# A graph layer on one core: windows of 180 message rows for each node tile in place of 192

## The chip, the cores and the metric

The kernel runs on one NeuronCore of a Trainium2 chip. The metric is the device time of one execution in microseconds (us); lower is better. The core has TensorE (PE in the rows; PEld is its weight load), VectorE (DVE), ScalarE (ACT), GpSimd (POOL) and SyncE (SP), and 16 DMA engines that move data between the main memory (HBM) and the on-chip memory.

## What is computed

One message-passing layer on a graph of 50,000 nodes with 160 features and 50,000 edges, and a LayerNorm behind it. The edges come sorted by their destination `dst`.

```python
h = silu(edge_scalars @ (Wfc1 / sqrt(16)));  w = h @ (Wfc2 / sqrt(64))
f0 = x0 @ Wl1_0 * a * inv8;   f1 = einsum('num,uv->nvm', x1, Wl1_1) * a * inv32
e0, e1 = f0[edge_src], f1[edge_src]           # gather by source
mid0..mid3 = products of w, e0/e1 and edge_attr_sh
n_k = segment_sum(mid_k, edge_dst) / clip(count, 1)   # mean by destination
conv = [scal @ Wl2_s, vec @ Wl2_v] * a * inv96;  alpha = scal @ Wa * a * inv96
out = layernorm(x + sc(x) + alpha * conv)     # sc: x times Wsc0, Wsc1
```

All arithmetic is float32. For the given inputs the 391 tiles of 128 nodes that hold nodes receive 128 edges each in the mean (standard deviation 11), and the fullest of them 160, counted from `dst`.

## The kernel before

The program has two stages, one after the other, and a start-up.

**Edge stage** (`edge_steps`): the edges go in 392 tiles of 128, two tiles to a step. GpSimd gathers the source rows (L548), TensorE transposes them and forms the weights and products, and VectorE writes a message of 163 numbers for each edge (gate, 160 features, a count of 1, and in the column `LABEL` the destination). Four tiles of messages at a time are stored to `rows` in HBM (L386). Behind the messages `rows` holds a pad of one window whose labels are -1.

**Window starts.** In the start-up GpSimd makes index tables and the pads (L505 to L528, `more_constants`, called after the second pair's gathers), and VectorE works out for each tile of 128 nodes at which row of `rows` its messages start. A flag (`prepare_flag`) sends the program to a slow general path if some tile has more than `WINDOW` messages or if `dst` isn't sorted; otherwise windows are used.

**Node stage** (`node_steps`): the nodes go in 98 groups of `GROUP = 4` tiles. For each group g:

- SP, `load_windows` (L413 to L425): it reads the four starts from `start_i` into registers (L413), waits until the window buffer is free (`agg_done` of the group four before; `RING = 4` buffers), and issues four DMAs (L422), one for each tile. A window is `WINDOW = WC_ROWS * WP` = 3 * 64 = 192 rows of messages, put into 64 partitions of three rows: tiles 0 and 1 into partitions 0 to 63 (`side(0)`), tiles 2 and 3 into partitions 64 to 127 (`side(1)`). Then it waits for `pre_ready` and `ra_ready` of the group four before and loads the node rows `xin` two groups ahead (`load_nodes`, L404). After every second group it waits for `fin_ready` and stores 8 tiles of results (L482).
- GpSimd: products `xa` of node rows and node attribute (L585, L589); when the group's windows have landed, the labels less the tile's first node, `lab` (L597); and the sum `res` (L608) of the group three before.
- VectorE: `hot` (L1082), a 0/1 matrix: which node of the tile a window row belongs to. A label outside the tile gives a row of zeros. Also the counts, coefficients, `pre` (L1044) and the statistics of the LayerNorm.
- TensorE: transposes of `xa` (L705); the sum by destination (L716), 24 products to a group, one for each tile and each of the three rows of a partition, contracting over the 64 partitions of `side(h)`; the self connection (L726, L728).
- ScalarE: `xt`, `agg` (L800), `std`, `fin` (L809).

The order on each engine is that of the loops; the engines meet in semaphores. The change touches `WP` (and with it `WINDOW`, the four loads L422, the products L716, the pads), `side`, and `more_constants`.

Of the kernel before, what the change touches and what calls it, by code (L numbers as in the profile page):

```python
# [47 lines left out]
GATE, CNT, LABEL = 0, 1 + D, 2 + D  # L48
SW = 2 + D
AW = 3 + D  # L50
RCNT, GRA = SW, SW + 1
WP = 64
WC_ROWS = 3
WINDOW = WC_ROWS * WP

# [19 lines left out]
def gnn_kernel(nc, table, x_g, src_t, dst_t, dst_rows, sh_t, ea_t, weights, out):  # L75
# [21 lines left out]
    with ExitStack() as ctx:  # L97
        def sb(name, shape, dt=F32):
            return ctx.enter_context(nc.sbuf_tensor(name, shape, dt))

        def sem(name):
            return ctx.enter_context(nc.semaphore(name))
# [14 lines left out]
        zeros = sb("zeros", [P, FILL, AW])  # L117
        pads = sb("pads", [WP, WC_ROWS, AW])

# [49 lines left out]
        win = sb("win", [P, RING, 2, WC_ROWS, AW])  # L169
# [47 lines left out]
        pads_set = sem("pads_set")  # L217
# [123 lines left out]
            return RING * i + (b - behind + 1)  # L341

        def side(h):
            return slice(h * WP, (h + 1) * WP)

        def block_rows(ap, first):

# [4 lines left out]
        def _(sp):  # L352
# [59 lines left out]
            def load_windows(i, b):  # L412
                _, firsts = nc.values_load_multi_w_load_instructions(  # L413
                    start_i[0:1, bass.ds((RING * i + b) * GROUP, GROUP)],
                    engines=[mybir.EngineType.SP], min_val=0, max_val=BASE + NP - P,
                    skip_runtime_bounds_check_because="a start is a count of edges, or the first "
                    "of a tile's own rows")

                if group_has(i, b, RING):
                    sp.wait_ge(agg_done, groups(i, b, RING))  # L420
                for k, first in enumerate(firsts):
                    sp.dma_start(win[side(k // 2), b, k % 2].rearrange("p c w -> p (c w)"),  # L422
                                 rows[bass.ds(first, WINDOW), :].rearrange(
                                     "(p c) w -> p (c w)", c=WC_ROWS)
                                 ).then_inc(win_in[b], 16)  # L425
# [67 lines left out]
        def _(pool):  # L493
# [10 lines left out]
            def more_constants():  # L504

                for ap, pattern, base, mult in (
                        (column[:], [[1, P]], 0, 0),
                        (tile_base[:], [[GROUP * P, NG], [P, 2]], 0, 0),
                        (bound[:], [[P * P, CH]], 0, P),
                        (node_base[:], [[P, NT]], BASE, 0),  # L510
                        (g_label[:], [[1, ROWS // P]], 0, ROWS // P),
                        (g_spare[:], [[0, 1]], NP, 1)):
                    nc.gpsimd.iota(ap.bitcast(I32), pattern=pattern, base=base,
                                   channel_multiplier=mult).then_inc(iotas_set, 1)
                pool.wait_ge(iotas_set, 6)
                nc.gpsimd.iota(tile_base[side(1), :].bitcast(I32),
                               pattern=[[GROUP * P, NG], [P, 2]], base=2 * P,
                               channel_multiplier=0).then_inc(iotas_set, 1)
                pool.wait_ge(iotas_set, 7)
                nc.gpsimd.memset(pads[:], 0.0).then_inc(pads_set, 1)  # L520
                nc.gpsimd.memset(later_mask[:], 1.0).then_inc(pads_set, 1)
                pool.wait_ge(pads_set, 2)
                nc.gpsimd.memset(pads[:, :, LABEL], -1.0).then_inc(pads_ready, 1)

                nc.gpsimd.affine_select(out=later_mask[:], in_=later_mask[:],
                                        compare_op=ALU.is_gt, fill=0.0, base=0,
                                        pattern=[[1, P]], channel_multiplier=-1
                                        ).then_inc(mask_ready, 1)  # L528
# [24 lines left out]
            def find_windows():  # L553

                pool.wait_ge(at_tile_i_ready, 1)
                for c in range(CH):
# [4 lines left out]
                    ).then_inc(picked_in, 16)  # L561

            edge_steps(pool, step, {(0, 1): more_constants, (1, 3): find_windows})

            pool.wait_ge(prepared, 1)
# [49 lines left out]
        def _(pe):  # L615
# [82 lines left out]
            def step(i, b):  # L698
# [8 lines left out]
                if group_alive(i, b, 1):  # L707
                    b1 = (b - 1) % 2

                    pe.wait_ge(hot_ready, groups(i, b, 1))  # L710
                    if group_has(i, b, 3):
                        pe.wait_ge(agg_ready, groups(i, b, 3))
                    for k in range(2):
                        for c in range(WC_ROWS):
                            for h in range(2):
                                last = nc.tensor.matmul(  # L716
                                    agg_ps[b1][:, 2 * h + k, 0:SW], hot[side(h), b1, k, c, :],
                                    win[side(h), (b - 1) % RING, k, c, 0:SW],
                                    start=c == 0, stop=c == WC_ROWS - 1)
                    last.then_inc(agg_done, 1)  # L720

                    pe.wait_ge(xt_out, groups(i, b, 1))
                    if group_has(i, b, 2):
                        pe.wait_ge(pre_ready, groups(i, b, 2))
                    for k in range(GROUP):
                        nc.tensor.matmul(sca_ps[:, k, :], xt[:, b1, k, :],  # L726
                                         wy[:, W_SA - W_Y0:W_SB - W_Y0], start=True, stop=True)
                    last = nc.tensor.matmul(scb_ps.rearrange("p k w -> p (k w)"),  # L728
                                            xt[:, b1, GROUP, :],
                                            wy[:, W_SB - W_Y0:WC - W_Y0], start=True, stop=True)  # L730
                    last.then_inc(sc_ready, 1)
# [463 lines left out]
```

## Time and profile before

| | us |
|---|---|
| median of 3 runs (lowest, highest) | 1144.48 (1143.96, 1147.09) |
| the profiled execution, device time | 1144.21 |
| its span, first to last instruction | 1142.4 |
| edge stage with start-up, to the first window load | 695 |
| node stage, from there to the end | 447 |

Device time and span differ by 1.8 us. The profile page gives for each engine the busy time and, in 40 slices of 28.6 us, the busy share in tenths. A view of waits lists for how long an engine stood idle and what it waited for. A timeline lists the instructions in order of time; for SP (in the rows SPq) it shows the DMAs that it issues and how long each issue occupied it. "MB" and "GB/s" are those of all 16 DMA engines. L422 is line 422 of the kernel.

### The profile page before, as it was taken

How to read it: one execution, taken by the hardware profiler on the slowest of the kernel's cores; microseconds unless marked ns; L12 is line 12 of the kernel's file. 1: busy time of each engine (PE TensorE's matmuls, PEld its weight loads, DVE VectorE, ACT ScalarE, POOL GpSimd, SP SyncE). 2: the span in 40 equal slices, each digit the busy share in tenths (PEclk: the TensorE clock that was granted, in tenths of full speed). 3: DMA queues.
4: the chain of work that ended last, by engine and by line, in shares of the span. 5: the costliest groups of instructions: out<-in, count | busy, mean ns of one | idle time of the engine just before them, and what ended most of it. 6: DMA issues, size and time to landing. Idle time of an engine off the chain costs nothing.

```text
span 1142.4 us, 29298 instructions
## 1 busy us (share of the span) xinstructions
PE 1024.2 (90%) x8726; PEld 941.3 (82%) x8726; DVE 908.3 (80%) x3171; ACT 640.4 (56%) x1865; POOL 759.4 (66%) x906
## 2 busy tenths in 40 slices
PE   4769999999999999999999998998888898998894
PEld 4759989989989998888888997887777787887783
DVE  4757877878787877777777876888988888988885
ACT  1324343434343434344343433888888898988887
POOL 6635656656656555666655662879887888878983
PEclk9879999999999999999999999999999999999997
DMA  5653333333333333333333433799989999998993
GB/s 160 151 135 98 107 99 101 94 104 103 97 99 107 99 97 98 105 98 98 98 97 95 112 98 121 218 267 273 270 260 262 282 281 264 283 264 258 271 276 136
DMA packets 88772, 186.64 MB, mean 163 GB/s; under 512 B 17831, under 2 KB 49895, under 8 KB 88616
## 3 DMA queue, kind: packets, MB, share of 16 engines
q1 hardware_dynamic: 69672, 152.17, 43.9%
q0 software_dynamic: 18944, 32.60, 14.0%
q8 instruction: 72, 1.18, 0.4%
q14 instruction: 84, 0.69, 0.2%
HBM read 119.75 MB, written 64.95 MB: 162 GB/s over the span
## 4 chain that ended last, share of the span: by engine, by line
PE 52%; issue 15%; POOL 14%; DVE 8%; another core or an unknown queue 5%; ACT 3%; DMA 2%; SPq 0%; DVEq 0%; POOLq 0%; ACTq 0%
PE ps L657 14%; PE ps L670 8%; PE ps L647 7%; POOL xa L589 6%; POOL xa L585 5%; PE ps L665 4%; PE ps L716 4%; PE ps L645 3%; PE ps L636 3%; PE ps L630 3%; PE ps L667 2%; POOL res L608 2%; PE ps L726 2%; PE ps L627 2%
## 5 line engine op out<-in xcount | busy, mean ns | idle before, releaser
L548 POOL DMA_INDIRECT gat<-table,src_now x392 | 377.1, 962 | 272.0 <-issue 135.5
L657 PEld LDWEIGHTS ps<-h_sb,wt 128*128 128x128 f32 x1568 | 204.3, 194 | 46.7 <-issue 38.8
L769 ACT ACTIVATE z<-ps 128x130 f32<-128x130 f32 x196 | 54.9, 280 | 325.2 <-PE ps L670 301.9
L657 PE MATMUL ps<-h_sb,wt 128*128 128x128 f32 x1568 | 213.3, 280 | 19.3 <-DVE mid L884 18.6
L716 PE MATMUL ps<-win,hot 64*128 64x162 f32 x2352 | 192.1, 309 | 0.0
L809 ACT ACTIVATE fin<-res,shift,rstd 128x160 f32<-128x160 f32 x392 | 172.1, 511 | 28.1 <-DVE shift L1090 25.9
L716 PEld LDWEIGHTS ps<-win,hot 64*128 64x128 f32 x2352 | 167.8, 189 | 16.7 <-issue 16.4
L608 POOL TENSOR_TENSOR res<-agg,pre 128x640 f32<-128x640 f32 x98 | 151.2, 1543 | 10.9 <-ACT agg L800 10.7
L670 PE MATMUL ps<-wy,mid 128*128 128x161 f32 x784 | 151.4, 316 | 0.0
L881 DVE TENSOR_TENSOR mid<-ps,e_sb 128x256 f32<-128x256 f32 x196 | 82.1, 419 | 85.0 <-remote 46.0
L1082 DVE TENSOR_TENSOR hot<-column,lab 128x768 f32<-128x768 f32 x98 | 135.3, 1381 | 1.0 <-issue 0.5
L762 ACT ACTIVATE e_sb<-ps 128x384 f32<-128x384 f32 x196 | 97.5, 498 | 67.7 <-PE ps L647 65.5
L800 ACT ACTIVATE agg<-ps,coef 128x160 f32<-128x160 f32 x392 | 121.6, 396 | 22.3 <-DVE coef L1075 22.3
L907 DVE SCALAR_TENSOR_TENSOR msg<-ps,sha,z 128x161 f32<-128x161 f32 x392 | 132.9, 381 | 0.3 <-issue 0.3
L1044 DVE TENSOR_TENSOR pre<-ps,xin 128x512 f32<-128x512 f32 x196 | 86.6, 482 | 42.3 <-PE ps L728 41.6
L647 PE MATMUL ps<-t_sb,wt 128*128 128x256 f32 x392 | 118.9, 386 | 0.0
L750 ACT ACTIVATE t_sb<-ps 128x384 f32<-128x384 f32 x196 | 95.7, 488 | 38.6 <-PE ps L630 26.0
L670 PEld LDWEIGHTS ps<-wy,mid 128*128 128x128 f32 x784 | 114.1, 192 | 0.0
L726 PE MATMUL ps<-wy,xt 128*128 128x128 f32 x784 | 113.9, 288 | 0.0
L589 POOL TENSOR_TENSOR xa<-xin 128x512 f32<-128x512 f32 x98 | 113.1, 1154 | 0.0
L705 PE MATMUL ps<-ident,xa 128*128 128x128 f32 x490 | 72.5, 279 | 43.7 <-POOL xa L589 41.6
L726 PEld LDWEIGHTS ps<-wy,xt 128*128 128x128 f32 x784 | 95.3, 192 | 17.4 <-issue 15.1
(98 smaller groups left out, 1880.1 us busy)
## 6 DMA issues: line engine op xcount, KB each, us to landing
win<-rows SPq DMA_DIRECT2D x392, 122.2 KB, 3.9
rows<-msg SPq DMA_DIRECT2D x98, 326.0 KB
xin<-x_g SPq DMA_DIRECT2D x98, 322.0 KB, 5.0
out<-fin SPq DMA_DIRECT2D x49, 640.0 KB, 5.5
gat<-table,src_now POOLq DMA_INDIRECT x392
eas<-ea_t SPq DMA_DIRECT2D x5, 512.0 KB
wt<-weights SPq DMA_DIRECT2D x1, 945.5 KB
shs<-sh_t SPq DMA_DIRECT2D x1, 752.0 KB
```

Source lines behind the costliest of these rows:

```text
L548: pool.indirect_dma_start(out=gat[:, n, 0:XW], out_offset=None, in_=table, in_offset=bass.IndirectOffsetOnAxis(ap=src_now[:, n:n + 1], axis=0)
L589: nc.gpsimd.tensor_tensor(xa[:, b0, 0:GROUP, :], xin[:, n, :, 1:1 + P], xin[:, n, :, 0:1].broadcast_to([P, GROUP, P]), ALU.mult).then_inc( ...
L608: nc.gpsimd.tensor_tensor(res[:, slot], agg[:, b3], pre[:, b3], ALU.add).then_inc(res_ready, 1)
L647: nc.tensor.matmul(e_ps[:, 1:3, :].rearrange("p s e -> p (s e)"), wt[:, W_E1:W_E1 + P], t_sb[:, b1, 1:3, :].rearrange("p s e -> p (s e)"), ...
L657: last = nc.tensor.matmul(w_ps[:, c, :], wt[:, w:w + P], h_sb[:, b1, :], start=True, stop=True)
L670: last = nc.tensor.matmul(y_ps[:, s, 1 + MUL0:YW], mid[:, b2, 2 + s, :], wy[:, W_Y1 - W_Y0:W_SA - W_Y0], start=True, stop=True)
L716: last = nc.tensor.matmul(agg_ps[b1][:, 2 * h + k, 0:SW], hot[side(h), b1, k, c, :], win[side(h), (b - 1) % RING, k, c, 0:SW], start=c == ...
L726: nc.tensor.matmul(sca_ps[:, k, :], xt[:, b1, k, :], wy[:, W_SA - W_Y0:W_SB - W_Y0], start=True, stop=True)
L800: last = nc.scalar.activation(agg[:, b0, k, :], agg_ps[b0][:, k, 1:1 + D], ACT.Copy, scale=coef[:, b0, k:k + 1])
L809: last = nc.scalar.activation(fin[:, past, k, :], res[:, past, k, :], ACT.Identity, bias=shift[:, past, k:k + 1], scale=rstd[:, past, k:k ...
L907: last = nc.vector.scalar_tensor_tensor(out=msg[:, 2 * j3 + s, 0:1 + D], in0=y_ps[:, s, 0:Y_C], scalar=sha[:, j3, s, 0:1], in1=z[:, b1, s, :],
L1082: nc.vector.tensor_tensor(hot[:, b0].rearrange("p k c e -> p (k c) e"), column[:].unsqueeze(1).broadcast_to([P, 2 * WC_ROWS, P]), lab[:, b ...
```

## The change

A window gets 180 rows in place of 192: `WP` becomes 60, so 60 partitions of three rows. The second half still starts at partition 64 (`HALF`). Partitions 60 to 63 and 124 to 127 of the window buffers are written by no load any more; their labels are set to -1 once, since `lab` and `hot` are still worked out for all 128 partitions. The products contract over 60 rows. The limit of the flag becomes 180.

```diff
@@ -49,7 +49,8 @@
 SW = 2 + D
 AW = 3 + D
 RCNT, GRA = SW, SW + 1
-WP = 64
+HALF = 64
+WP = 60
 WC_ROWS = 3
 WINDOW = WC_ROWS * WP
 
@@ -341,7 +342,7 @@
             return RING * i + (b - behind + 1)
 
         def side(h):
-            return slice(h * WP, (h + 1) * WP)
+            return slice(h * HALF, h * HALF + WP)
 
         def block_rows(ap, first):
 
@@ -519,7 +520,8 @@
                 pool.wait_ge(iotas_set, 7)
                 nc.gpsimd.memset(pads[:], 0.0).then_inc(pads_set, 1)
                 nc.gpsimd.memset(later_mask[:], 1.0).then_inc(pads_set, 1)
-                pool.wait_ge(pads_set, 2)
+                nc.gpsimd.memset(win[:, :, :, :, LABEL], -1.0).then_inc(pads_set, 1)
+                pool.wait_ge(pads_set, 3)
                 nc.gpsimd.memset(pads[:, :, LABEL], -1.0).then_inc(pads_ready, 1)
```

## Rows read from the trace of the kernel before

**Rows 1.** The profile page: span, and busy tenths in 40 slices
```profile
span 1142.4 us, 29298 instructions
PE   4769999999999999999999998998888898998894
DVE  4757877878787877777777876888988888988885
ACT  1324343434343434344343433888888898988887
POOL 6635656656656555666655662879887888878983
DMA  5653333333333333333333433799989999998993
```
**Rows 2.** Busy time of each engine by stretch: edge stage, node stage, last stretch
```profile
300.00:500.00 200.00, 191.78 (x1487) 180.53 (x1487) 158.68 (x595) 80.60 (x238) 120.03 (x149) 1.00 0.37 101
765.00:1105.00 340.00, 303.06 (x3070) 269.28 (x3070) 299.75 (x949) 297.44 (x868) 284.81 (x315) 0.99 0.96 270
1105.00:1142.40 37.40, 20.45 (x208) 17.93 (x204) 22.97 (x82) 29.16 (x84) 19.18 (x19) 0.83 0.49 167
```
**Rows 3.** Waits, all engines, 765 to 1105 us: total, times, longest
```profile
POOL lab L597 <- DMA win<-rows: 46.1, 44, 2.9
PE ps L705 <- POOL xa L589: 36.8, 36, 2.5
DVE pre L1044 <- PE ps L728: 31.3, 37, 1.5
```
**Rows 4.** Waits of SP's queue, 765 to 1105 us: all there are
```profile
SPq L404 <- DVE pre L1044: 3.7, 11, 0.6
SPq L482 <- ACT fin L809: 0.8, 2, 0.4
```
**Rows 5.** Timeline of SP where nothing holds it back: start us, us
```profile
718.30 2.44 SPq L422 DMA_DIRECT2D win<-rows  x4
720.84 0.53 SPq L404 DMA_DIRECT2D xin<-x_g  x1
721.87 2.44 SPq L422 DMA_DIRECT2D win<-rows  x4
```
**Rows 6.** Timeline of SP in mid node stage
```profile
944.70 3.25 SPq L422 DMA_DIRECT2D win<-rows  x4
948.06 0.51 SPq L404 DMA_DIRECT2D xin<-x_g  x1
949.09 2.46 SPq L422 DMA_DIRECT2D win<-rows  x4
951.64 0.53 SPq L404 DMA_DIRECT2D xin<-x_g  x1
952.22 0.42 SPq L482 DMA_DIRECT2D out<-fin  x1
953.15 3.03 SPq L422 DMA_DIRECT2D win<-rows  x4
...
961.43 3.26 SPq L422 DMA_DIRECT2D win<-rows  x4
...
969.88 3.23 SPq L422 DMA_DIRECT2D win<-rows  x4
```
**Rows 7.** Line L422, 765 to 1105 us: issue ns min/median/max
```profile
L422 SPq DMA_DIRECT2D win<-rows x315: 468/471/1920, 765.1 to 1104.4; - x158
```
**Rows 8.** DMA view, 765 to 1105 us: packets by size, loads and stores
```profile
DMA packets 42238, 91.97 MB, mean 270 GB/s; under 512 B 6925, under 2 KB 27089, under 8 KB 42182
win<-rows SPq DMA_DIRECT2D x315, 122.2 KB, 4.0
xin<-x_g SPq DMA_DIRECT2D x79, 322.0 KB, 4.9
out<-fin SPq DMA_DIRECT2D x39, 640.0 KB, 5.6
```
**Rows 9.** Groups by line, PE, 750 to 1100 us: busy us, mean ns
```profile
L716 PEld LDWEIGHTS ps<-win,hot 64*128 64x128 f32 x1946 | 138.4, 188 | 13.8 <-issue 13.6 <-DVE hot L1082 0.2
L726 PEld LDWEIGHTS ps<-wy,xt 128*128 128x128 f32 x648 | 78.8, 192 | 14.4 <-issue 12.8 <-ACT xt L792 1.6
```
**Rows 10.** Page, products with nearly the same columns: busy us, mean ns
```profile
L716 PE MATMUL ps<-win,hot 64*128 64x162 f32 x2352 | 192.1, 309 | 0.0
L670 PE MATMUL ps<-wy,mid 128*128 128x161 f32 x784 | 151.4, 316 | 0.0
```
**Rows 11.** Timeline of GpSimd in the start-up: start us, us
```profile
8.54 0.95 POOL L548 DMA_INDIRECT gat<-table,src_now  x1 [0.30 <-issue]
...
12.14 0.50 POOL L520 MEMSET pads<- 64x489 f32 x1
12.59 0.42 POOL L521 MEMSET later_mask<- 128x128 f32 x1
13.06 0.10 POOL L523 MEMSET pads<- 64x3 f32 x1
13.12 1.29 POOL L525 TENSOR_SCALAR_AFFINE_SELECT later_mask<-later_mask 128x128 f32<-128x128 f32 x1
14.37 0.18 POOL L538 COPY src_now<-srcs 128x4 int32<-128x4 int32 x1
15.36 1.02 POOL L548 DMA_INDIRECT gat<-table,src_now  x1 [0.81 <-POOL src_now L538]
```
**Rows 12.** DMA issues of other shapes, by line: ns min/median/max
```profile
L399 SPq DMA_DIRECT2D start_row<-starts_dram x1: 266/266/266, 61.8 to 61.8; - x1
L386 SPq DMA_DIRECT2D rows<-msg x98: 332/332/833, 38.0 to 708.6; - x98
L365 SPq DMA_DIRECT2D heads_i<-dst_rows x1: 973/973/973, 3.3 to 3.3; - x1
```
**Rows 13.** Timeline of SP in the start-up, and the page's size of `wt`
```profile
1.28 0.42 SPq L359 DMA_DIRECT2D wt<-weights  x1
...
3.28 0.97 SPq L365 DMA_DIRECT2D heads_i<-dst_rows  x1
...
wt<-weights SPq DMA_DIRECT2D x1, 945.5 KB
```

## The prediction

> **What bounds the kernel now.** Read the page's slices first [rows 1]. For 24 of 40 slices, the edge stage, TensorE is at 9 and the DMA engines at 3; after that the DMA row stands at 8 to 9 to the end and all four engines stand at 8 or so. The change touches the edge stage only in its start-up, so the node stage is what matters. The view by stretch [rows 2] says the same in numbers: from 765 to 1105 us the 16 DMA engines are busy 0.96 of the time and move 270 GB/s, TensorE is busy 303 of 340 us, VectorE 300, ScalarE 297, GpSimd 285. No engine is full, so look at what they wait for [rows 3]: the longest wait is GpSimd's, 46.1 us for window loads, and the next ones (the transposes for `xa`, `pre` for the self connection) come behind it in the loop. So the windows are late. Why? Either SP issues them late because a buffer is not free, or SP itself is late, or the DMA engines are. The waits of SP's queue [rows 4] rule out the first: in 340 us SP waited 4.5 us for other engines. SP is therefore occupied with issuing all the time.
>
> Its timeline shows with what. Where nothing holds it back [rows 5], a group takes 721.87 - 718.30 = 3.57 us: four window loads 2.44 us, one node load 0.53 us, and about half a microsecond between the node load and the next window, in which the starts are read into registers. With the store of results (every second group) it is 953.15 - 949.09 = 4.06 us [rows 6]. The mean, 3.82 us, is SP's own work for a group. The real pace is 79 node loads, one a group [rows 8], in 340 us: 4.30 us. The missing 0.48 us is in the issues themselves: the median issue of a window load takes 471 ns but some take up to 1920 [rows 7], and the long quartets (3.25, 3.03, 3.26 and 3.23 us against 2.44) stand right behind the store of 640 KB [rows 6, 8]. I read this as SP pushing against full DMA queues, at a DMA share of 0.96. So two things in series set the pace: SP's issuing, 3.82 of 4.30 us, and the DMA engines, which take the rest. What the change does to either decides; the four computing engines have 11 to 16% of slack.
>
> **The change part by part.** The sum is made against the profiled execution, 1144.21 us, 0.3 us below the median of the runs.
>
> *Products over 60 rows.* The 24 products of a group keep their number and their columns. Does a shorter contraction make them faster? With 64 rows the weight load takes 188 ns, with 128 rows 192 [rows 9]; the product 309 ns for 162 columns over 64 rows, 316 for 161 over 128 [rows 10]. Halving the rows gave at most 7 ns, so a sixteenth less gives nothing. `hot` and `lab` keep their shapes, all 128 partitions.
>
> *The memset of the labels and its wait.* One GpSimd instruction of 128x24 numbers between L521 and L523. Its neighbours take 0.10 us (64x3) and 0.42 us (128x128) [rows 11]; I take 0.25. GpSimd has the gather of 15.36 us queued behind it, and the edge pipeline is being filled at that time, so nothing surely hides it: 0.1 to 0.5 us, once.
>
> *The window loads, bytes.* Each of the 392 loads loses 4 of 64 packets of three message rows (122.2 KB / 64 = 1956 bytes [rows 8]). For a group that is 16 packets, 31.3 kB of 4 * 122.2 + 322 + 320 KB = 1158 kB, 2.7% of the traffic. If time went by bytes, that is 31.3 kB at 270 GB/s = 0.116 us a group. But a load is done when its last engine is done, and a packet is not split. 64 packets over 16 engines are four for each; 60 packets leave at least one engine with four, and if each engine takes an equal number, 15 engines keep four and one gets none. Then the queues of 15 engines hold just what they held before, and they set the end. Bounds: 0 and -0.116 us a group. I take 0, since an equal division is the plain way to cut 60 equal packets, and a varied one is the rival below.
>
> Here a page bears on it. The Trainium skill, "DMA: Bandwidth & Descriptors", section on why a DMA increments its semaphore by 16, says that the descriptor generator picks the largest number of engines up to 16 that divides the row counts, and that with HWDGE these are always the lowest-numbered ones. By it the 60 rows go to 15 fixed engines and the 16th is idle for every window, so the gain from bytes would be 0; the opposite result, -0.116 us a group, is that of counting bytes. No row of this trace shows single DMA engines.
>
> *The window loads, issue.* This is the cost that the trace doesn't show: what SP needs to issue a load whose 60 rows don't divide by 16. All loads and stores of the node stage have 64 or 128 rows. Nearest rows [rows 12]: the one DMA of a single row took 266 ns, the message stores in an idle queue 332; the one DMA whose count is no multiple of 16, `heads_i` with 392 pieces, took 973 ns. So the price lies between 332 - 266 = 66 ns less and 973 - 420 = 553 ns more, where 420 is that of a plain issue within a burst (the store's in [rows 6]). `heads_i` was issued two microseconds behind a load of 945 KB [rows 13], and behind the 640 KB store the quartets wait as well, so much of its 973 ns may be waiting. I take +40 ns, near the 64-row load, because all else of the load is the same, and keep both ends. The same page says that the issuing sequencer itself writes the remaining increments when fewer than 16 engines take part; that would be an addition to each issue, and no run here has its price.
>
> *What of it reaches the end.* 4 * 0.04 = 0.16 us a group on SP. SP already stands still for 0.48 us a group against full queues; when it comes later, the queues have drained further and it stands less. That cover isn't perfect, since the standstill falls mostly on every second quartet and the DMA share is 0.96 and not 1. I take three quarters as covered: 0.04 us * 98 groups = 4 us. Without the cover it would be 16 us.
>
> Sum: 1144.2 + 0.25 (memset) + 0 (products) + 0 (bytes) + 4 (issue) = 1148.5, and its own range 1142 to 1154: the issue price from 0 to 60 ns with half to all of it covered, and a little from the engine or two with less to do.
>
> **The rivals.**
>
> *Bytes count.* If the DMA engines are slow together, because the memory or the way into the chip's memory is shared, then 2.7% less traffic helps whichever engine it is taken from. For it: the DMA share is full at 270 GB/s, whatever limits it. Against it: the equal division above, and that GpSimd, VectorE and TensorE need 285 to 303 us of the 340 themselves. Price: 0.116 us * about 90 groups that run at full DMA share = 10.4 us, so 1134. It can't go much further: SP's 3.82 us a group stays.
>
> *A dear issue (slower).* If issuing 60 rows costs over 0.48 / 4 = 0.12 us more than 64, SP's own work passes the present pace of 4.30 us and the cover is used up; from there each 0.1 us of price costs 0.4 us a group, 39 us in all. Place: L422, 392 times. At 0.2 us more: 3.82 + 0.80 = 4.62 us a group plus some standstill, 0.4 us * 98 = 39 us, so 1183. At the upper bound of 0.55 us: (2.20 - 0.48) * 98 = 169 us, 1313. For it: `heads_i`. Against it: 973 ns can be a full queue.
>
> *The change doesn't do what it says.* With a limit of 180 rows the flag would send the program to the general path if a tile had more. The fullest tile of these inputs has 160, so windows are used; I leave 1 in 100.
>
> **How the numbers follow.** My forecast, nothing from the bytes and a small, mostly covered price of the issue: 0.53, at 1148. Bytes count: 0.24, 1131 to 1141. A dear issue: 0.20, from 1155 up, half of it above 1178. Others: 0.03. A measurement of this kernel can tell about 0.3%, 3.4 us, from no change: 1141.1 to 1147.9 is the same. Of the forecast's 0.53 I put 0.35 there, 0.16 above and 0.02 below; bytes count gives 0.22 faster and 0.02 the same; the dear issue 0.20 slower. With the others: faster 0.25, same 0.38, slower 0.37. The range runs from the bytes case's 1132 to 1178 in the dear case; about 0.1 is left out above and 0.04 below. The forecast's own range is 1142 to 1154.
>
> **What the profile of the changed kernel would show.** The median issue of L422: 471 ns now; 500 to 530 if my price is right, over 600 for the dear issue, the same or less for none. The pace of node loads: 4.30 us now; 4.34 by the forecast, 4.19 if bytes count, 4.5 and up if the issue is dear. The quartets right behind a store should shrink by about what the others grow. DMA share: by the forecast the mean falls by about a sixteenth of the windows' part, since one engine idles, though nothing gets faster; if bytes count, GB/s stay near 270 and the share near 0.96. The wait for `win` grows with SP, or shrinks if bytes count. The products stay at 309 ns. I am wrong if the median issue is unchanged and the pace still moves: then the engines' queues, not SP, carry the change.

## The result, and the profile after

The changed kernel takes 1103.98 us (median of 4 runs, 1100.88 to 1113.02) against 1144.5; the ratio is 0.966, with a 95% interval of 0.962 to 0.970. That is 40 us faster, where the prediction said 1148 and gave 1132 as the low end. The profiled execution has a span of 1104.4 us against 1142.4.

The page after, to be laid against [rows 1]:

```profile
span 1104.4 us, 29299 instructions
PE   4669999999999999999999999899999999999994
DVE  4658777887887777877778788599999999999995
ACT  2224433434343343444344333389999999999997
DMA  5553333333333333333333333489999999999993
```

The edge stage is as long as before: the first window load is issued at 696.3 us, 695.4 before. All of the gain is in the node stage, where TensorE, VectorE and ScalarE went from 8 tenths to 9. The same in numbers, by stretch (us, then busy us of PE, PE's weight load, DVE, ACT and POOL, TensorE's clock, DMA share, GB/s), 765 to 1060 us, first the changed kernel:

```profile
765.00:1060.00 295.00, 286.39 (x2966) 257.82 (x2967) 282.12 (x914) 282.71 (x837) 265.79 (x305) 1.00 1.01 292
```

The waits of the same stretch, all engines, and then those of SP's queue (in all, times, longest). Before, GpSimd's wait for windows was 42.8 us in this stretch, and 46.1 in the longer one of [rows 3]:

```profile
POOL lab L599 <- DMA win<-rows: 24.7, 33, 1.7
PE ps L707 <- POOL xa L591: 6.7, 7, 1.4
...
SPq L478 <- DVE ra L1061: 8.5, 19, 0.7
SPq L423 <- PE ps L718: 1.8, 2, 0.9
```

And what SP needs for an issue (ns min/median/max), window loads and node loads of the changed kernel in that stretch:

```profile
L423 SPq DMA_DIRECT2D win<-rows x304: 327/328/1402, 765.9 to 1058.7; - x152
L405 SPq DMA_DIRECT2D xin<-x_g x76: 362/362/562, 768.4 to 1059.4; - x76
```

Here is the surprise. A window load of 60 partitions occupies SP for 328 ns, one of 64 for 471 [rows 7]. And the node load behind it, which the change does not touch, fell too. Its line before, same stretch:

```profile
L404 SPq DMA_DIRECT2D xin<-x_g x68: 508/531/1608, 766.5 to 1056.4; - x68
```

531 to 362 ns. The count in these two lines is the pace: 68 groups in 295 us before, 4.34 us each; 76 after, 3.88. The difference, 0.46 us a group, over some 90 groups is the whole 40 us.

One instruction of SP got slower. Before each group SP reads the four window starts into registers, and this read stands behind the node load and the store. Before and after, same stretch (ns min/median/max):

```profile
L413 SPq TENSOR_LOAD <-start_i x68: 293/301/307, 767.0 to 1057.4; - x68
L414 SPq TENSOR_LOAD <-start_i x76: 483/492/812, 765.2 to 1056.4; - x76
```

SP's timeline after, to be laid against [rows 6]:

```profile
809.00 1.90 SPq L423 DMA_DIRECT2D win<-rows  x4
811.00 0.36 SPq L405 DMA_DIRECT2D xin<-x_g  x1
811.41 0.42 SPq L483 DMA_DIRECT2D out<-fin  x1
812.53 2.39 SPq L423 DMA_DIRECT2D win<-rows  x4
```

A quartet that nothing holds back takes 1.90 us and not 2.44. For a group SP saves 0.54 us on the windows and 0.17 on the node load, and loses 0.19 on the read of the starts: 0.52 in all, from 3.82 to 3.30 us. Measured from start to start it is the same: a group with a store takes 812.53 - 809.00 = 3.53 us, against 4.06 in [rows 6]. Most quartets behind a store are still long (2.39 here), and the standstill is 3.88 - 3.30 = 0.58 us a group, against 0.52 before in this stretch. The DMA share is now 1.01 at 292 GB/s, where 0.96 at 270 looked full: the 270 GB/s were no ceiling.

The theory from here on, **theory 1**: the kernel was bound by SP's issuing, as predicted, and the change made the issue cheaper, not dearer. Rivals: the DMA engines have less to do (fewer bytes, or one engine left out), or the shorter products.

### The profile page after: what moved, and what is told of

The parts are those of the page before. It is cut to its first block, busy times and chain, and to the rows that moved or that the text cites. A ratio compares the mean times of both kernels' runs of the same rounds, so it can differ in the third digit from the quotient of the medians.

```text
span 1104.4 us, 29299 instructions
## 1 busy us (share of the span) xinstructions
PE 1015.5 (92%) x8726; PEld 940.0 (85%) x8726; DVE 899.9 (81%) x3171; ACT 636.6 (58%) x1865; POOL 752.1 (68%) x907
## 4 chain that ended last, share of the span: by engine, by line
PE 67%; issue 10%; DVE 7%; another core or an unknown queue 6%; POOL 5%; ACT 2%; DMA 2%; SPq 0%; DVEq 0%; POOLq 0%; ACTq 0%
PE ps L659 14%; PE ps L718 11%; PE ps L672 8%; PE ps L649 6%; PE ps L728 6%; PE ps L667 4%; PE ps L707 3%; PE ps L638 3%; PE ps L632 3%; PE ps L647 3%; POOL xa L591 2%; PE ps L669 2%; PE ps L629 2%; DVE mid L886 1%
## 5 line engine op out<-in xcount | busy, mean ns | idle before, releaser
L718 PE MATMUL ps<-win,hot 60*128 60x162 f32 x2352 | 190.7, 307 | 2.4 <-ACT agg L802 0.3
L718 PEld LDWEIGHTS ps<-win,hot 60*128 60x128 f32 x2352 | 167.5, 188 | 20.2 <-DVE hot L1084 10.9
L1084 DVE TENSOR_TENSOR hot<-column,lab 128x768 f32<-128x768 f32 x98 | 147.7, 1508 | 0.5 <-issue 0.5
L591 POOL TENSOR_TENSOR xa<-xin 128x512 f32<-128x512 f32 x98 | 106.2, 1084 | 0.0
L667 PE MATMUL ps<-wy,mid 128*128 128x130 f32 x392 | 81.1, 289 | 13.6 <-DVE msg L909 13.4
```

The source lines that it names most:

```text
L591: nc.gpsimd.tensor_tensor(xa[:, b0, 0:GROUP, :], xin[:, n, :, 1:1 + P], xin[:, n, :, 0:1].broadcast_to([P, GROUP, P]), ALU.mult).then_inc( ...
L667: nc.tensor.matmul(y_ps[:, :, 0:1 + MUL0], mid[:, b2, 0, :], wy[:, 0:W_YB - W_Y0], start=True, stop=True)
L718: last = nc.tensor.matmul(agg_ps[b1][:, 2 * h + k, 0:SW], hot[side(h), b1, k, c, :], win[side(h), (b - 1) % RING, k, c, 0:SW], start=c == ...
L1084: nc.vector.tensor_tensor(hot[:, b0].rearrange("p k c e -> p (k c) e"), column[:].unsqueeze(1).broadcast_to([P, 2 * WC_ROWS, P]), lab[:, b ...
```

## The experiments

The first runs (the first bursts, loads alone, time given back, fewer bytes) were made on one chip, the rest on two others, on which the kernel before takes 1157 us instead of 1144. Times are therefore compared as ratios to the kernel before in the same session.

**Bursts of DMAs by themselves.** The disputed price, measured at the end of the kernel before, when nothing else runs:

```diff
+BENCH = [(n, 0) for n in (64, 60, 56, 48, 40, 32, 52, 44, 128, 120, 112, 96, 100, 64, 60, 4, 1)]
...
+            for count, rest_rows in BENCH:
+                for n in range(8):
+                    if count > 0:
+                        sp.dma_start(scratch[0:count, n, :],
+                                     rows[0:3 * count, :].rearrange("(p c) w -> p (c w)", c=3)
+                                     ).then_inc(bench_in, 16)
+                burst += 8
+                sp.wait_ge(bench_in, 16 * burst)
```

> The kernel before, and behind its last store SP issues bursts of eight equal loads (1956 bytes to a partition, fixed address) into a scratch buffer, one burst each for 64, 60, 56, 48, 40, 32, 52, 44, 128, 120, 112, 96, 100, 64, 60, 4 and 1 partitions, and waits for each burst. It measures the disputed price of an issue by itself. Theory A, the price goes with 16 engines taking part: within a burst the counts that divide by 16 (64, 48, 32, 128, 112, 96) cost about 420 to 470 ns each, and those that don't (60, 56, 52, 44, 120, 100) about 330, as the 60-row loads of the changed kernel did (328 against 468). Theory B, the price goes with the number of partitions: it falls smoothly from 128 to 1, and 60 and 64 lie within 10 ns of each other. The time from a burst's first issue to the end of its wait tells what fewer engines cost in bandwidth.

SP's timeline, one line for each burst of eight (start, us from the first to the end of the last issue), for 64, 60, 48, 32 and 128 partitions, then 120, 96 and 100:

```profile
1143.47 4.97 SPq L498 DMA_DIRECT2D scratch<-rows  x8
1150.64 3.50 SPq L498 DMA_DIRECT2D scratch<-rows  x8
...
1163.68 3.77 SPq L498 DMA_DIRECT2D scratch<-rows  x8
...
1176.33 3.56 SPq L498 DMA_DIRECT2D scratch<-rows  x8
...
1193.86 3.68 SPq L498 DMA_DIRECT2D scratch<-rows  x8
1201.75 3.52 SPq L498 DMA_DIRECT2D scratch<-rows  x8
...
1219.01 3.59 SPq L498 DMA_DIRECT2D scratch<-rows  x8
1226.53 2.98 SPq L498 DMA_DIRECT2D scratch<-rows  x8
```

Issue by issue inside a burst, behind the first of it: 64 partitions 597 ns, 128 432, 32 422, 48 424, 60 406, 56 388, 52 372, 44 349, 40 333, 4 295, 1 252. Neither theory A nor B holds as written. Without the 64 there is a gentle slope: counts that divide by 16 cost 422 to 432 whether they are 32 or 128, and the others less, in the order of the largest number up to 16 that divides them (60: 15, 56: 14, 52: 13, 44: 11, 40: 10). That slope is worth 20 ns for 60 rows. And 64 stands by itself, 170 ns above.

The bursts also bear on how rows are shared. From one burst's start to the next, 96 partitions took 7.5 us, 128 took 7.9, and 100 took 9.3: longer than 128 with a fifth less to move. Shared equally, 100 rows give ten engines 10 packets each, and 128 rows give sixteen engines 8. The mean DMA share was 0.78 in the burst for 128 and 0.49 for 100, which fits idle engines. Equal shares do not explain 120: fifteen engines would have 8 packets each, as with 128, and yet the burst took 9.1 us at a share of 0.76.

**What makes 64 dear.** Again bursts of eight behind the end, with other sources, sizes, places and directions.

```diff
+BENCH = [(("plain", 64),), (("plain", 60),), (("strided", 64),), (("strided", 60),),
+         (("short", 64),), (("short", 60),), (("high", 64),), (("high", 60),),
+         (("plain", 64), ("plain", 128)), (("plain", 60), ("plain", 128)),
+         (("plain", 62),), (("plain", 63),), (("plain", 54),), (("plain", 80),), (("plain", 16),),
+         (("strided", 128),), (("store", 64),), (("store", 60),), (("store", 128),)]
...
+                    kind, count = kinds[n % len(kinds)]
+                    to, source = piece(kind, count, n)
+                    sp.dma_start(to, source).then_inc(bench_in, 16)
```

> Bursts of eight DMAs behind the end of the kernel before, as in the first bench, to find what makes the 64-partition load dear (597 ns against 406 for 60, 432 for 128 and 424 for 48). In this order: 64 and 60 partitions with 1956 contiguous bytes each from one contiguous stretch; the same with gaps in the source; the same with 652 bytes; the same into partitions from 64 up; 64 and 128 in turn; 60 and 128 in turn; 62, 63, 54, 80, 16; 128 with gaps; stores of 64, 60 and 128. Theory A, the number 64 itself: all 64-partition DMAs cost near 600 whatever their source, size and direction. Theory B, the contiguous source of this size is cut up in a costly way: 64 with gaps costs near 430. Theory C, the price is work left behind that the next issue waits for: in the 64/128 series the 128s are the dear ones, in the 60/128 series neither is. Counts with few engines (62 on 2, 63 on 9, 54 on 9) should be cheap to issue and, if engines share equally, slow to land.

In the code "strided" is a source with gaps, "short" is 652 bytes to a partition, "high" goes into partitions from 64 up. In this order: plain 64 and 60; 64 and 128 in turn, 60 and 128 in turn; 62; 63; stores of 64 and 60:

```profile
1154.19 4.97 SPq L519 DMA_DIRECT2D scratch<-rows  x8
1161.35 3.50 SPq L519 DMA_DIRECT2D scratch<-rows  x8
...
1206.52 4.54 SPq L519 DMA_DIRECT2D scratch<-rows  x8
1215.40 3.49 SPq L519 DMA_DIRECT2D scratch<-rows  x8
1222.75 10.73 SPq L519 DMA_DIRECT2D scratch<-rows  x8
1244.50 2.83 SPq L519 DMA_DIRECT2D scratch<-rows  x8
...
1277.87 5.00 SPq L519 DMA_DIRECT2D rows<-scratch  x8
1284.65 3.67 SPq L519 DMA_DIRECT2D rows<-scratch  x8
```

The bursts of 652 bytes have issues of 597 and 406 ns as well. Theory A holds: every 64-partition DMA behind another costs 592 to 597 ns (the stores 596 to 604), with or without gaps, 1956 or 652 bytes, in either half, load or store. Theory C holds too, for a part: a 64 costs 472 ns when a 128 is ahead of it, and then the 128 behind it costs 592, where a 128 behind a 128 costs 432; 60 and 128 in turn cost 442 and 378. So a 64 leaves a price for whatever is issued behind it. It also has one of its own when nothing is ahead: the first of a burst took 472 to 501 ns, for 60 partitions 328 to 416. That is what the kernel showed: 0.14 us on each window load, 0.17 on the node load. Why this one count is dear stays open; nothing here looks inside the issue.

The 62 is a warning. It is cheap at first (258 to 315 ns), but its largest divisor up to 16 is 2: from the fifth on each issue stood for 2.3 us, and the burst took 21.8 us where the one for 60 took 6.5.

**The loads alone.** Loads of 60 partitions, products over 64 again:

```diff
+        def full(h):
+            return slice(h * HALF, (h + 1) * HALF)
...
-                                    agg_ps[b1][:, 2 * h + k, 0:SW], hot[side(h), b1, k, c, :],
-                                    win[side(h), (b - 1) % RING, k, c, 0:SW],
+                                    agg_ps[b1][:, 2 * h + k, 0:SW], hot[full(h), b1, k, c, :],
+                                    win[full(h), (b - 1) % RING, k, c, 0:SW],
...
-                nc.gpsimd.memset(win[:, :, :, :, LABEL], -1.0).then_inc(pads_set, 1)
+                nc.gpsimd.memset(win[:], -1.0).then_inc(pads_set, 1)
```

> One part of the change alone: the loads bring 180 rows into 60 partitions, but the products contract over 64 partitions again (the four idle ones hold -1 and match no node, so the output is the same). Theory 1, SP's issue is what got cheaper: 1104 us, as the changed kernel. Theory 2, the shorter products brought it: back towards 1144 us.

1110.28 us, ratio 0.970 (0.966 to 0.975). Its one extra cost is visible in GpSimd's timeline of the start-up:

```profile
12.72 3.35 POOL L526 MEMSET win<- 128x3912 f32 x1
```

This memset puts off the first gathers: the one that ran at 15.3 us runs at 18.8. 1110.3 less about 3.4 is 1107, the changed kernel within noise. The products bring nothing (308 ns against 307 in the changed kernel).

**SP's time given back.** The changed kernel with waits on SP that are long fulfilled:

```diff
                 for k, first in enumerate(firsts):
+                    for _ in range(3):
+                        sp.wait_ge(weights_in, 32)
...
+                for _ in range(4):
+                    sp.wait_ge(weights_in, 32)
                 sp.dma_start(xin[:, n].rearrange("p k w -> p (k w)"), block_rows(x_g, g)
```

> The changed kernel, with three waits on a semaphore that has long been reached ahead of each window load on SP, and four ahead of each node load, about 47 ns each: this gives SP back the 0.14 us for each window load and 0.17 us for each node load that the change took away, 0.75 us a group, and changes no transfer. Theory 1, SP's issue time is the gain: 1135 to 1145 us. Theory 2, the gain is that of the DMA engines (fewer bytes, 15 of them): it stays at 1104 to 1110 us.

1135.39 us, ratio 0.993 (0.990 to 0.996). All transfers are those of the changed kernel, and 31 of the 40 us gained are gone. SP's timeline:

```profile
861.76 2.37 SPq L427 DMA_DIRECT2D win<-rows  x4
864.35 0.36 SPq L407 DMA_DIRECT2D xin<-x_g  x1
865.53 2.08 SPq L427 DMA_DIRECT2D win<-rows  x4
867.83 0.36 SPq L407 DMA_DIRECT2D xin<-x_g  x1
868.25 0.42 SPq L487 DMA_DIRECT2D out<-fin  x1
869.49 0.39 SPq L427 DMA_DIRECT2D win<-rows  x1
```

The waits were partly folded into other instructions, so they cost less than planned. And what the change took away was not the 0.75 us of the expectation but 0.52, since that sum has no term for the read of the starts. The unblocked steps are 3.77 - (2.37 - 2.08) = 3.48 us, and 3.96 with a store: 3.72 in the mean (not 3.9, as the expectation of a later run has it from a blocked step), 0.42 above the changed kernel's 3.30 and still 0.10 below the kernel before. The pace was 70 groups in 295 us, 4.21 us each: 0.33 above the changed kernel. So the run came out at the lower edge of what theory 1 said, for a reason that can be seen, and theory 2 (1104 to 1110) is out.

**Fewer bytes alone.** The kernel before, each packet without its first 30 numbers (they are left out of the sums):

```diff
-                    sp.dma_start(win[side(k // 2), b, k % 2].rearrange("p c w -> p (c w)"),
+                    sp.dma_start(win[side(k // 2), b, k % 2].rearrange("p c w -> p (c w)")[:, 30:],
-                                     "(p c) w -> p (c w)", c=WC_ROWS)
+                                     "(p c) w -> p (c w)", c=WC_ROWS)[:, 30:]
...
+                nc.gpsimd.memset(win[:], 0.0).then_inc(pads_set, 1)
```

> The kernel before with its 64-partition loads, but each packet leaves out the first 30 of its 489 numbers (6.1% fewer window bytes, as the change has 6.25% fewer; the gate and 29 features of the first of a partition's three rows are left out of the sum). Issue stays at 468 ns. Theory 1: SP still issues for 3.82 us a group, only the standing still can shrink: 1139 to 1145 us. Theory 2, bytes are what counts: 1104 to 1134 us.

1151.69 us, ratio 1.007 (1.005 to 1.009); less the same 3.35 us memset it is 1148, above both theories and no gain at all. The issues were as before (468 ns), but SP's register steps between the loads took 46 to 51 ns instead of 37 to 42, which makes about 0.04 us a group, or 4 us, and accounts for the rest. The DMA engines did have less to do: their share fell from 0.96 to 0.88, and a window landed 3.4 us after its issue instead of 4.0. The packets begin at other addresses, so this is not a clean cut of a sixteenth; but it gives the bytes no credit.

**The store off SP.** The kernel before, with the 49 stores issued by ScalarE behind `fin`:

```diff
-                    sp.wait_ge(fin_ready, groups(i, b, 8))
-                    sp.dma_start(block_rows(out, i * (RING // 2) + (b - 9) // 2),
...
+                    act.wait_ge(fin_ready, g6 + 1)
+                    act.dma_start(block_rows(out, g6 // 2),
```

> The kernel before with its 64-partition loads, but the 49 stores of results are issued by ScalarE instead of SP. That takes 0.49 us in every second group off SP (0.24 us a group of 3.82) and changes no byte. Theory 1, SP's issuing is what bound the kernel before: 1120 to 1132 us. Theory 2, the DMA engines bound it: 1140 to 1147 us, or slower by what ScalarE loses.

1145.64 us against 1156.56 in that session, ratio 0.991 (0.987 to 0.994): 11 us for 0.24 us a group of SP's time. In ratios, theory 1 said 0.979 to 0.989 and theory 2 0.996 to 1.002, so the result lies between the two. The direction is theory 1's, but the size is under half of what SP saves (0.24 * 98 = 24). The edit is not a clean one: the stores also go out two groups earlier and from a queue of ScalarE's. The windows still came late:

```profile
POOL lab L591 <- DMA win<-rows: 40.6, 40, 2.8
```

**48 partitions, without and with the waits on SP.** 144 rows a window; messages beyond them are left out, and the flag still allows 192.

```diff
-WP = 60
+WP = 48
...
-                                               scalar=float(WINDOW), in1=wrong_ps,
+                                               scalar=192.0, in1=wrong_ps,
```

> The changed kernel with 48 partitions of three rows for a window (144 rows; messages of a tile beyond the 144th are left out of the sums, and the flag still allows 192): 16 engines can share 48 rows equally, three packets each, and the count is not 64. Theory 1a, 64 is dear and anything else is not: issue in the kernel about 328 to 340, SP as cheap as with 60, and the time at or under 1104 us. Theory 1b, 15 engines are what is cheap to issue for: issue near 468 again; then only bytes can help, 1115 to 1144 us. If after the cheaper issue the DMA engines are the next bound, a quarter less window bytes gives up to 10 us more (1094); if TensorE at 97% busy is, it stays at 1100 to 1104.

1110.34 us, ratio 0.962 (0.958 to 0.966), the same as the changed kernel's on another of those two chips (0.962, below). Issue, the read of the starts, then the stretch 765 to 1060 us, then the waits:

```profile
L423 SPq DMA_DIRECT2D win<-rows x311: 315/316/1624, 764.3 to 1060.0; - x156
...
L414 SPq TENSOR_LOAD <-start_i x77: 293/301/413, 767.9 to 1057.7; - x77
...
765.00:1060.00 295.00, 291.51 (x3021) 263.15 (x3021) 284.74 (x930) 287.12 (x851) 291.03 (x310) 1.00 0.96 273
...
POOL lab L599 <- DMA win<-rows: 0.2, 1, 0.2
```

48 divides by 16, and the issue is as cheap as with 60: what the change escaped is the number 64, and not the sharing among all 16 engines. The read of the starts is back at 301 ns; it took 301 with 64 partitions as well, and 492 to 494 with 60, 56 and 63, the counts that don't divide by 16. So SP's own work is 0.28 us a group less than with 60 partitions. With that and a fifth less of window bytes the wait for windows ended (0.2 us in all), but TensorE was busy 291.5 of 295 us and GpSimd 291.0, and these are the next bound. With the waits on SP added:

> Windows of 48 partitions (messages of a tile beyond the 144th are left out), with the same extra waits on SP as in the run with fillers. There 60-partition windows gave 1135 us with SP's own work at 3.9 us a group, while the kernel before gave 1144 with 3.8. If the 9 us between them are the DMA queues' (one engine free, fewer bytes), then three packets for each of 16 engines in place of four for each of 15 give more of the same: 1115 to 1130 us. If DMA traffic plays no part while SP is this slow: 1133 to 1138.

1127.34 us, ratio 0.974 (0.969 to 0.979), against 0.993 for 60 partitions with the same waits. The expectation compares traffic with traffic, but SP's own work differs too. A group with a store, where nothing held it:

```profile
854.97 2.00 SPq L427 DMA_DIRECT2D win<-rows  x4
...
858.64 3.03 SPq L427 DMA_DIRECT2D win<-rows  x4
```

That is 3.67 us, against 3.96 with 60 partitions and the same waits: 0.29 us less, most of it the read of the starts (302 ns against 491). Over 98 groups it is 28 us, and the two runs, made on different chips, are 0.019 or 22 us apart. So the difference needs no lighter DMA queues, and the run does not show that they help.

Laid side by side, SP's own time for a group with a store orders the runs (the stretch 765 to 1060 us; the ratio is that of the run):

| kernel | SP, unblocked, us | pace, us a group | ratio |
|---|---|---|---|
| before | 4.06 | 4.34 | 1 |
| 60 partitions and waits | 3.96 | 4.21 | 0.993 |
| 48 partitions and waits | 3.67 | 4.04 | 0.974 |
| 60 partitions (pace of the first run) | 3.53 | 3.88 | 0.966, again 0.962 |
| 48 partitions | 3.25 | 3.83 | 0.962 |

Down to the changed kernel each 0.1 us of SP's time is worth 0.6 to 0.7% of the whole time, whatever rows the loads bring; the last row has met TensorE and GpSimd. The runs come from three chips, so the ratios and not the times are to be compared. The kernel with the stores on ScalarE doesn't fit: there 0.24 us a group brought 0.9%.

**56 and 63 partitions.** With 56 the program took 5035 us:

> The changed kernel with 56 partitions of three rows (168 rows a window, which still holds the fullest tile of 160): 14 engines with four packets each. Theory 1: issue as cheap as with 60; 14 engines still have four packets a load, so 1098 to 1106 us, the same as 60 within noise. If bytes counted beside the issue: 1096 or below.

It had gone the general path, by the flag. The last tile of nodes receives the 176 edges that fill up the last tiles of edges, and 168 rows don't hold them; 180 do, by four. With the flag held at 192:

> The changed kernel with 56 partitions, 168 rows, and a flag that still allows 192: the only tile with more than 168 messages is the last, where 176 filling edges go that belong to no node; some of them are left out of its sum. 14 engines, four packets each. Issue about 330 ns, time within 4 us of the changed kernel in the same session: the engines with work have as much as before, and TensorE is at 97%. If bytes counted: 5 us or more faster.

1112.06 us, ratio 0.961 (0.956 to 0.966), and on the window path again. The changed kernel itself, same session:

> The changed kernel itself, for comparison on the same chip: a ratio of 0.966 to the kernel before, as in the first measurement.

1115.08 us, ratio 0.962 (0.957 to 0.967). A fifteenth fewer window bytes changed nothing; shared equally, each working engine has four packets in both. And 63:

> The changed kernel with 63 partitions of three rows (189 rows), which is not 64 either and was as cheap to issue in the bursts (322 ns), but lands on 9 engines with seven packets each if the engines share equally. Theory 1, with the sharing: SP's own work stays small, and the nine engines have 28 window packets a group instead of 16, at 0.12 us each 1.4 us a group more: 1200 to 1260 us, with long blocked issues. If only the issue price mattered: 1100 to 1110.

1163.72 us, ratio 1.007 (1.004 to 1.010), and SP's waits:

```profile
SPq L478 <- DVE ra L1061: 46.1, 57, 1.2
SPq L423 <- PE ps L718: 26.7, 42, 0.9
```

The issue was the cheapest of all (278 ns) and SP had time to wait, 73 us in 295. The node load landed 9.2 us after its issue, against 6.2 in the changed kernel, and GpSimd waited 40.9 us for windows: the loads came late, as they would with seven packets on each of nine engines, and the loop waited for them. I had said 1200 to 1260. The price was smaller; I had charged 0.12 us for each packet, and why it cost less here no run shows.

## Why the prediction was wrong

- **What bounds the kernel: right for SP, and shown; not shown for the rest.** Giving SP its time back took back 31 of 40 us, and SP's own time orders the runs. The rest of the pace I laid to full DMA queues. It stayed at 0.5 to 0.6 us a group while the DMA share went from 0.88 (fewer bytes) to 1.01 (changed kernel), so what SP stands against is open. The share itself misled me: I expected it to fall with an idle engine, and it rose from 0.96.
- **Products, 0: right.** 309 to 307 ns, and loads alone gave the gain.
- **Memset, 0.25 us: right in size** (0.24), but hidden: the next gather started at 15.33 us against 15.36 [rows 11], and the line shows why, with the instruction behind it now shorter by as much.

```profile
12.95 0.24 POOL L523 MEMSET win<- 128x24 f32 x1
13.25 1.01 POOL L525 MEMSET pads<- 60x3 f32 x1
13.30 1.07 POOL L527 TENSOR_SCALAR_AFFINE_SELECT later_mask<-later_mask 128x128 f32<-128x128 f32 x1
```

- **Bytes, 0: right as far as the runs tell.** 56 and 60 partitions are the same, the cut bytes gave nothing, and the bursts of 100 and 62 rows fit equal shares on fewer engines; that of 120 rows was longer than equal shares make it. The rule of the Trainium skill, "DMA: Bandwidth & Descriptors", section on why a DMA increments its semaphore by 16, fits all of these but the 120; which engines are used no run shows.
- **Issue, +40 ns: this is the step that failed**, in its sign. It is -140 ns on each window load. Two terms that my sum did not have come with it: -169 ns on each node load and +190 on each read of the starts. In all SP saves 0.52 us a group, where I had 0.16 more. I had bounded it by 66 ns less and 553 more, and -140 is outside. The fault lies ahead of the bounds: I took the 64-row load as the normal price and asked only what could make 60 rows dearer. The same view of the kernel before said otherwise. In a burst, 128 partitions cost 420 [rows 6], and yet the 64-row load cost 471 [rows 7], with idle time for SP's register work between. The node load cost 531 ns behind a window, but six of them alone in the start-up took less:

```profile
62.09 3.06 SPq L404 DMA_DIRECT2D xin<-x_g  x6
```

  0.51 us each, and of the six issues four took 431 to 433 ns, the first 358 and one 764. And the one 64-partition DMA of the start-up, `rows<-pads`, took 629 ns; it takes 461 in the changed kernel, with 60. Three rows pointed at the shape, and I read none of them that way; I let `heads_i`, which also had a big load ahead of it, point the other way.
- **Cover, three quarters: this failed too.** Of the 0.52 us that SP saves, the pace got 0.46; of the 0.42 given back, 0.33; of the 0.24 with the store moved, 0.11. Over 98 groups SP saves 51 us, and 40 reach the end. With the right price my sum would still have let only a quarter through: 0.13 * 98 = 13 us, 1131 in place of 1104. The standstill that was to give way moved little: 0.52 us a group before, 0.58 in the changed kernel, 0.49 with the waits.
- **The cap was right.** I said the four engines need 285 to 303 of 340 us; TensorE's 303 is 3.84 us a group, and the pace stopped at 3.88. With 48 partitions it stopped at 3.83.
- **The rivals.** "A dear issue" had the right place and the wrong sign. "The change doesn't do what it says" I gave 1 in 100 for a fullest tile of 160. The tile that counts has 176, from filling edges; it still fits into 180, but with four partitions fewer the kernel takes 5035 us.

## What to carry to other kernels

When a queue's own issues are the bound, list the cost of an issue by shape and look for the one that is out of line before asking what a new shape may cost. An instruction's price may lie on the one behind it: here 0.17 us was saved on a load that the change never touched, and 0.19 lost on a register read that it never touched either. So measure a queue's work from start to start of the loop, and not by adding up the issues. When two variants are to differ in traffic alone, check that first. And a row count should be tried against its divisors: 60 was a good number; 63 was a bad one in the kernel, and 62 in the bursts.

## What was not expected of the hardware

A DMA over exactly 64 partitions cost SP 468 ns (apart from others, in the kernel) to 597 (in a burst) to issue, and made the next one dearer; 60 cost 328 to 442, 48 cost 316 to 424, 128 cost 332 to 432. For 64, the two sizes, both directions and both places tried made no difference. Otherwise the price in a burst roughly followed the largest number up to 16 that divides the rows, from 252 ns for one row to about 425 for 16. With 62 rows, four loads of 121 kB went through, and each further issue then stood for 2.3 us.

SP's register read behind the node load and the store took 301 ns in the kernels with windows of 64 and 48 partitions, and 492 to 494 with 60, 56 and 63, though no DMA just ahead of it had changed. No run shows why.
